# A graph layer on one core: additions behind chained operations, and two of ten step rows made by VectorE

## The reference

```python
q = (embeds[rows] @ qW).reshape(e, HEADS, dh)      # rows = src, cols = dst
k = (embeds[cols] @ kW).reshape(e, HEADS, dh)
v = (embeds[cols] @ vW).reshape(e, HEADS, dh)
scores = jnp.clip(jnp.einsum('ehd,ehd->eh', q, k), -10.0, 10.0)
exp_s = jnp.exp(scores)
norms = jax.ops.segment_sum(exp_s, rows, num_segments=nvar)[rows]
w = exp_s / (norms + 1e-08)
res = jax.ops.segment_sum(w[:, :, None] * v, rows, num_segments=nvar).reshape(nvar, d)
return embeds + res
# and outside: x = _layernorm(x + that, axis=-1)
```

## Time and profile before

| | |
|---|---|
| timed runs | 1259.94 us median of 3 (1259.18 to 1260.97) |
| profiled execution | span 1256.5 us; the page gives no other time for it |
| VectorE (DVE) busy | 1028.6 us, 82% |
| TensorE matmul (PE) busy | 976.0 us, 78% |
| GpSimd (POOL) busy | 866.1 us, 69% |
| ScalarE (ACT) busy | 656.4 us, 52% |
| gathers | 855, 986 ns mean |
| chain that ended last | DVE 25%, ACT 21%, POOL 20%, PE 17%, issue 13% |

### The profile page before, as it was taken

How to read it: one execution, slowest core, us unless ns; L and a number is a source line. 1 busy time by engine, 2 the same in 40 slices (tenths; PEclk the granted TensorE clock), 3 DMA queues, 4 the chain that set the end, 5 groups by cost and what they waited for, 6 DMA issues and landing times.

```text
span 1256.5 us, 23019 instructions
## 1 busy us (share of the span) xinstructions
PE 976.0 (78%) x6512; PEld 886.1 (71%) x6513; DVE 1028.6 (82%) x3053; ACT 656.4 (52%) x1469; POOL 866.1 (69%) x887
## 2 busy tenths in 40 slices
PE   8876788678776888776898777899777788888870
PEld 6765787568755788666888666788676777777760
DVE  8999998899898999889999789999668655555557
ACT  6852693249832499422899232799424322222225
POOL 1217776767777777777777777777777777777752
PEclk9996687659885599866799775799769755555555
DMA  6202222222222222222222222222622222222222
GB/s 174 88 10 76 77 80 69 74 64 75 78 73 70 70 75 79 76 74 68 77 77 80 78 75 70 79 77 78 151 79 80 77 78 78 79 78 77 77 61 77
DMA packets 67241, 98.34 MB, mean 78 GB/s; under 512 B 33127, under 2 KB 53204, under 8 KB 67134
## 3 DMA queue, kind: packets, MB, share of 16 engines
q0 software_dynamic: 41040, 84.10, 24.7%
q1 hardware_dynamic: 26094, 12.94, 3.9%
HBM read 89.77 MB, written 7.22 MB: 77 GB/s over the span
## 4 chain that ended last, share of the span: by engine, by line
DVE 25%; ACT 21%; POOL 20%; PE 17%; issue 13%; DVEq 2%; DMA 1%; SPq 0%; POOLq 0%; ACTq 0%
POOL kv L508 20%; ACT steps_m L719 14%; PE ps_r L662 5%; DVE acc L1127 4%; PE ps_q L648 4%; ACT oneh L773 3%; PE ps_a L631 3%; ACT onehT L767 2%; DVE steps_m L849 2%; DVE prod L1146 2%; DVE place_m L1013 2%; DVE place_m L1017 2%; DVEq L423 2%; PE ps_r L545 1%; DMA kv<-kv_table,dst_s 1%
## 5 line engine op out<-in xcount | busy, mean ns | idle before, releaser
L508 POOL DMA_INDIRECT kv<-kv_table,dst_s x855 | 843.4, 986 | 324.0 <-issue 315.8
L648 PE MATMUL ps_q<-qt,onehT 128*128 x1760 | 321.8, 348 | 108.6 <-ACT onehT L767 97.1
L648 PEld LDWEIGHTS ps_q<-qt,onehT 128*128 128x128 f32 x1760 | 291.3, 254 | 139.5 <-issue 139.0
L662 PE MATMUL ps_r<-wv,oneh 128*128 128x100 f32 x1752 | 322.5, 350 | 70.4 <-DVE wv L1156 69.9
L662 PEld LDWEIGHTS ps_r<-wv,oneh 128*128 128x128 f32 x1752 | 295.2, 258 | 87.0 <-DVE wv L1156 82.9
L719 ACT ACTIVATE steps_m<-iota_f,pos_t 125x254 f16<-125x254 f32 (+4 forms) x794 | 312.5, 502 | 16.4 <-PE ps_b L631 8.7
L1127 DVE TENSOR_TENSOR acc<-acc,ps_r 128x100 f32 x876 | 220.6, 252 | 62.9 <-issue 24.8
L767 ACT ACTIVATE onehT<-ps_t 128x640 f32<-128x640 bf16 x176 | 124.5, 707 | 183.2 <-PE ps_t L674 176.4
L760 ACT ACTIVATE wv<-clipped 128x20 f32<-128x20 f32 x176 | 39.4, 224 | 333.9 <-DVE clipped L1174 333.6
L631 PE MATMUL ps_a<-steps_m,place_m 125*128 125x254 f16 (+4 forms) x1504 | 183.9, 279 | 29.8 <-ACT steps_m L719 29.8
L1146 DVE TENSOR_TENSOR prod<-ps_q,kv 128x480 f32<-128x480 f32 x176 | 114.7, 652 | 107.3 <-DMA kv<-kv_table,dst_s 103.8
(11 more groups left out here) (208 smaller groups left out, 602.2 us busy)
## 6 DMA issues: line engine op xcount, KB each, us to landing
kv<-kv_table,dst_s POOLq DMA_INDIRECT x855
kv_table<-kv SPq DMA_DIRECT2D x7, 672.0 KB, 3.7
acc<-in_x_dram SPq DMA_DIRECT2D x6, 336.0 KB, 7.8
steps_m<-in_x_dram SPq DMA_DIRECT2D x6, 336.0 KB, 6.3
out_dram<-kv SPq DMA_DIRECT2D x6, 336.0 KB
dst_i<-in_dst_dram SPq DMA_DIRECT2D x1, 415.0 KB
src_i<-in_src_dram SPq DMA_DIRECT2D x1, 346.7 KB
acc<-in_x_dram SPq DMA_DIRECT2D x1, 288.0 KB, 4.6
```

Of the source, the lines that this page charges most:

```text
L508: nc.gpsimd.indirect_dma_start(kv[:, nm, u, :], None, kv_dram, bass.IndirectOffsetOnAxis(ap=dst_s[:, n * U + u:n * U + u + 1], axis=0)).th ...
L648: last = nc.tensor.matmul(ps_q[nm % 2][:, u * D:(u + 1) * D], onehT[:, nm % 2, u * P:(u + 1) * P], qt[:, bass.ds(blks[u], 1), :].rearrange ...
L662: last = nc.tensor.matmul(to, oneh[:, nm % 2, u, :], wv[:, nm % 2, u, :], start=True, stop=True)
```

## The change

In iterations with ranking pieces the pieces now run inside `tiles`: VectorE does product, weighing, reduction, one-hot and clip without any addition, then the pieces, and after each `link`'s instruction is issued, and before the wait for it, it issues one of the five additions (`add_one`); those left over come at the end. The register load of the block numbers moves ahead of the product in every iteration. `pair` and `select` wait only for what they read, over three buffers. `pay` moves into `count`, behind the counts' semaphore. The names of the pieces are spread over the iterations without `pay`. In iterations with a sort unit the third addition moves ahead of the clip, the fourth behind it, the fifth behind the one-hot. For groups 1 to 5 ScalarE makes eight Sign rows; VectorE makes the other two by a compare of 2 x (T + 1) elements (T is 204, 224, 243, 253, 253), payloads are doubled there too, and pos_h is made in each group.

```diff
+    KG = 2
@@ plan
-                    + ["pair0", "pair1", "pair2", "pay", "count", "base0", "base1", "bounds"]
+                    + ["pair0", "pair1", "pair2", "count", "base0", "base1", "bounds"]
...
             for k in range(ranked):
-                m = plan_iters(m, 1)
-                for name in names[at[k]:at[k + 1]]:
-                    PLAN.append(("piece", name, g))
+                m = plan_iters(m, 1, g, mid=names[at[k]:at[k + 1]])
@@ TensorE, unit
-                        steps = theta_d[:, vm, :, j] if g == 0 and j < KD else theta[:, vm, j, 0:w]
+                        steps = theta[:, vm, j, 0:w]
+                        if j < (KG if g else KD):
+                            steps = theta_g[:, vm, 0:w, j] if g else theta_d[:, vm, :, j]
@@ ScalarE
+            nc.scalar.activation(iota_g[:, :, :], iota_f[:, 0:TMAX + 1].unsqueeze(2).to_broadcast([P, TMAX + 1, KG]),
+                                 ACT.Copy)
...
-                for j in range(KD if g == 0 else 0, SU):
+                for j in range(KG if g else KD, SU):
@@ VectorE
-            def link(ins):
+            behind = [iter(())]
+
+            def step(ins):
 
                 own[0] += 1
                 ins.then_inc(s_own, 1)
+                return own[0]
+
+            def add_one():
+
+                for add_up, u in itertools.islice(behind[0], 1):
+                    add_up(u)
+
+            def link(ins):
+
+                step(ins)
+                add_one()
                 dve.wait_ge(s_own, own[0])
@@ pay
-                if g == 0:
-                    for part_of in (upper, lower):
-                        twice = part_of.rearrange("p (v c) -> p v c", c=SU)[:, :, 0:KD]
-                        link(nc.vector.tensor_scalar(twice, twice, 2.0, None, ALU.mult))
+                for part_of in (upper, lower):
+                    twice = part_of.rearrange("p (v c) -> p v c", c=SU)[:, :, 0:KG if g else KD]
+                    link(nc.vector.tensor_scalar(twice, twice, 2.0, None, ALU.mult))
@@ pair
+                a = 1 + 3 * i
                 if i == 0:
-                    link(nc.vector.tensor_scalar(rank_u[:, 0:K], bin_u[:, 0:K], 0.0, None, ALU.mult))
-                for d in range(1 + 3 * i, 4 + 3 * i):
...
+                    nc.vector.tensor_scalar(rank_u[:, 0:K], bin_u[:, 0:K], 0.0, None, ALU.mult)
+                known = compare(a)
+                add_one()
+                known_2 = compare(a + 1)
+                if i:
+                    dve.wait_ge(s_own, known)
+                    known = add(a)
+                add_one()
+                known_3 = compare(a + 2)
+                dve.wait_ge(s_own, max(known, known_2))
+                known = add(a + 1)
+                add_one()
+                dve.wait_ge(s_own, max(known, known_3))
+                known = add(a + 2)
+                add_one()
+                dve.wait_ge(s_own, known)
@@ count
                 nc.vector.tensor_copy(cnt[:, :], cnt_f[:, :]).then_inc(s_cnt, 1)
+                pay(g)
                 dve.wait_ge(s_pre, g + 1)
@@ base
+                if i:
+                    link(last)
+                else:
+                    add_one()
@@ select
+                def add(k):
+                    dve.wait_ge(s_own, max(chosen[0], chosen[k]))
+                    chosen[0] = step(nc.vector.tensor_tensor(rows(0), rows(0), rows(k), ALU.add))
+                    add_one()
+
+                chosen[i] = step(nc.vector.tensor_tensor(...))
+                add_one()
+                if i > 1:
+                    add(i - 1)
+                if i == 6:
+                    add(i)
+                    dve.wait_ge(s_own, chosen[0])
@@ own_position
-                if g == 0:
-                    link(nc.vector.tensor_scalar(pos_h[:, :], t, 0.5, None, ALU.add))
+                link(nc.vector.tensor_scalar(pos_h[:, 0:C], t, 0.5, None, ALU.add))
@@ unit
+                else:
+                    w = TS[g] + 1
+                    nc.vector.tensor_tensor(theta_g[:, vm, 0:w, :], iota_g[0:EP, 0:w, :],
+                                            pos_h[:, here].unsqueeze(1).to_broadcast([EP, w, SU])[:, :, 0:KG],
                                             ALU.is_le)
@@ tiles
+                if there(m - 2):
+                    blks = blocks_of(mybir.EngineType.DVE, m - 2)
                 multiply()
                 weigh()
                 if there(m - 2):
-                    blks = blocks_of(mybir.EngineType.DVE, m - 2)
                     dve.wait_ge(s_res, m - 2 + 1)
+                if mid:
+                    reduce()
+                    build()
+                    clip()
+                    behind[0] = iter([(add_up, u) for u in range(U)])
+                    for piece, g in mid:
+                        piece(g)
+                    for _, u in behind[0]:
+                        add_up(u)
+                    return
                 add_up(0)
                 reduce()
                 add_up(1)
                 build()
+                add_up(2)
                 clip()
-                add_up(2)
+                add_up(3)
                 if sorts:
-                    unit(*sorts[0], between=lambda i: add_up(3 + i))
+                    unit(*sorts[0], between=lambda i: None if i else add_up(4))
```

More of the change, by code:

```diff
@@ L3 @@
 from contextlib import ExitStack
+import itertools
 def gnn(nc, x, src, dst, qW, kW, vW, out):
@@ L85, in last_use, with plan_iters @@
         return MB + 2 * (k - MB) + 1 if k < MB + PAIRS // U else k + PAIRS // U
-    def plan_iters(m, count, units=()):
+    def plan_iters(m, count, g=0, units=(), mid=()):
         units = list(units) + [()] * (count - len(units))
-        PLAN.append(("iters", m, 0, units))
+        PLAN.append(("iters", m, g, units, mid))
         return m + count
@@ L131, in plan @@
             for k in range(ranked):
-                m = plan_iters(m, 1)
-                for name in names[at[k]:at[k + 1]]:
-                    PLAN.append(("piece", name, g))
+                m = plan_iters(m, 1, g, mid=names[at[k]:at[k + 1]])
             at = shares(units, count - ranked)
-            PLAN.append(("iters", m, g, [tuple(range(V0[g] + a, V0[g] + b)) for a, b in zip(at, at[1:])]))
+            m = plan_iters(m, count - ranked, g, [tuple(range(V0[g] + a, V0[g] + b)) for a, b in zip(at, at[1:])])
             PLAN.append(("piece", "lower", g))
-            m = plan_iters(m + count - ranked, 1)
+            m = plan_iters(m, 1)
             for name in ("differ", "turn", "choice"):
@@ L163, in gnn @@
         iota_s = sb("iota_s", [P, P, SU], f16)
-        pos_h = sb("pos_h", [EP, GC[0]], f16)
+        pos_h = sb("pos_h", [EP, CMAX], f16)
+        iota_g = sb("iota_g", [P, TMAX + 1, KG], f16)
+        theta_g = sb("theta_g", [EP, 2, TMAX + 1, KG], f16)
         iota_u = sb("iota_u", [P, NB], u16)
@@ L386, in follow @@
                 elif what[0] == "iters":
-                    _, m0, g, units = what
+                    _, m0, g, units, names = what
                     for k, vs in enumerate(units):
@@ L390, in follow @@
                         sorts = [(g, v - late, (v - late) % 2) for v in vs if V0[g] <= v - late < V0[g + 1]]
-                        tiles(m0 + k, (m0 + k) % R, sorts if unit else ())
+                        tiles(m0 + k, (m0 + k) % R, sorts if unit else (), [(pieces[p], g) for p in names if p in pieces])
                 elif what[2]:
@@ new lines, in add @@
+                def add(d):
+                    return step(nc.vector.tensor_tensor(rank_u[:, d * K:C], rank_u[:, d * K:C],
+                                                        same_u[:, d % 3, d * K:C], ALU.add))
+                a = 1 + 3 * i
+                if i == 0:
+                    nc.vector.tensor_scalar(rank_u[:, 0:K], bin_u[:, 0:K], 0.0, None, ALU.mult)
[5 more added lines that the diff above has]
+                    known = add(a)
@@ L1209, in tiles @@
                 else:
-                    add_up(3)
                     add_up(4)
-            follow(dve, tiles, unit, {"count": count, "table": table, "own": own_position, "pay": pay,
+            follow(dve, tiles, unit, {"count": count, "table": table, "own": own_position,
                                       "bounds": bounds, "choose": choose, "differ": differ, "pick": pick,
```

44 lines of the change are left out of this document (22 added, 22 removed).

## The result

The changed kernel takes 1249.83 us (median of 6, 1248.31 to 1251.50) against 1260.29 us for the kernel before in the same set (6 runs, 1256.80 to 1260.97): ratio 0.9924, 95% interval 0.9911 to 0.9936. Run again with the experiments it took 1251.98 us, ratio 0.9932 (0.9910 to 0.9954). The profiled execution took 1251.4 us with a span of 1249.6. Every execution whose span is listed took 1.8 us more than it, so the profiled one of the kernel before, with a span of 1256.5, took some 1258.3. The forecast was 1264.

What follows compares the result with a forecast made beforehand. Until 605 us VectorE's iteration time was taken to set the clock, afterwards GpSimd's gathers at 1.25 us each. Ranking -4.3, sort stages +5 and between stages +3 gave +4 on 1259.94: 1264 us, range 1249 to 1275.

Steps and rivals of the forecast that it cites:

- Ranking: VectorE's ranking iterations before 605 us: register load, additions and chains together save 4.3 us.
- (a): Ranking iterations before 605: the register load ahead of the product is no longer covered, net +16.5 us.
- (b): Ranking iterations before 605: additions placed in the waits of chained operations cost less, net -11.1 us.
- (c): Ranking chains before 605: removed waits, shorter pairs and moved payload, less new doublings and pos_h, net -9.7 us.
- Sort stages: Three sort stages before 605: VectorE's compare and closer additions, less waiting for ScalarE, add 5 us.
- slow step of four: First group's sort: strided matmuls 0.17 against 0.08 start to start; doubling would add 0.5 us per unit on TensorE, just hidden.
- Between the stages: After each sort: wait for cum_a stays, perhaps 0.3 shorter, and the register load costs more; three groups, +3 us.
- Rival 3: Sort stages and cum_a: ScalarE's relief reaches further, wait shrinks 1 to 2 us per group; -4, 1260 us; chance 0.20.
- what the change does to VectorE before 605 moves the end one for one: Before 605 us VectorE's time sets the clock, so its +4 us goes straight to the kernel's end.
- floor for stops: GpSimd's gaps above 0.30 us between gathers total 27 us at most, so no more can be won.
- a fixed 31 us: All 855 gathers: time taken beyond 0.95 us each, mean 986 against 0.95, 31 us in sum.
- the prediction's own key: If GpSimd's gaps above 0.30 vanish, the load or additions step failed; if they shrink with those right, sort stages were mis-sized.

Runs made afterwards that it cites:

- e3: Changed kernel with the register load back behind the weighing in iterations with ranking pieces: 1258.82 us (0.9983).
- e2: Kernel before with only the compare, its doubled payloads and pos_h; additions and register load as before: 1264.06 us (1.0024).
- e1: Changed kernel without the compare, ScalarE making all ten Sign rows; additions and register load stay changed: 1259.73 us (0.9987).
- e5: Changed kernel with the register load behind the weighing in ranking iterations and the selections chained again: 1242.12 us (0.9856).
- e10: Changed kernel, old sort-iteration addition order, weights copied to q's PSUM bank, TensorE waiting for the weighing, which still reads SBUF: 1277.29 us (1.0135).
- e14: Changed kernel, old sort-iteration addition order, weights copied to the transposes' PSUM bank, no new wait, weighing still reads SBUF: 1258.80 us (0.9982).
- e9: Changed kernel, old sort-iteration addition order, weighing reads weights copied to q's PSUM bank, TensorE waiting for the weighing: 1263.28 us (1.0024).
- e13: Changed kernel, old sort-iteration addition order, weighing reads weights copied to the transposes' PSUM bank, no new wait: 1239.80 us (0.9833).

## Why the prediction was wrong, step by step

**Up to iteration 71** VectorE was to lose 4 us; it won 9.7 (512.4 to 502.7 behind the first gather).

- Start: nothing forecast, -1.3 measured: the first product stands 8.8 us behind the first gather, not 10.1. What moved it is not settled.
- Ranking: -4.3 forecast, -5.4 measured. Its parts held nearly. The additions stand 0.40 apart. The load costs 1.33 or 1.34 us behind pieces that end in a chain (1.15 was taken), 1.07 behind serial additions (1.0), mostly nothing or 0.47 elsewhere. e3, which takes only the load back, has 12.9 us less in these iterations: so (a), forecast at +16.5, came to +12.9, and (b) and (c) together to -18.4 where -20.8 was forecast. Two errors cancelled in part. In the whole program the product's idle time has 46.5 us of issue in 49 places:

```profile
  DMA kv<-kv_table,dst_s: 91.2, 34
  issue: 46.5, 49
  PE ps_q L652: 14.2, 10
```

- Sort stages: +5 forecast, +4.1 measured. 5.8 per iteration of the fourth was forecast, 5.76 came, and the compare of 508 elements takes 0.42 us, as estimated. The strided matmuls cost nearly nothing: two of them start 0.24 us ahead of the plain ones (0.12 each), and the eight plain ones stand 0.11 apart (TensorE, fourth sort stage):

```profile
646.47 0.40 PE L635 MATMUL ps_a<-theta_g,place_m 125*128 125x254 f16 x2
646.71 1.04 PE L635 MATMUL ps_a<-steps_m,place_m 125*128 125x254 f16 x8
```

  The forecast had carried the slow step of four in the earlier trace rows over to a step of two, 0.5 us more on TensorE per unit; that was wrong, but hidden, and cost the sum nothing. The Trainium skill (Advanced Engine Details and Errata, SBUF Cachelines) asks for at least two hits on a 16-byte line. By that rule a step of two, with four hits, is free, and these rows agree; a step of four, with two, is not shown free by the earlier trace rows.

- **Between the stages: +3 forecast, -7.0 measured. This is the first step that failed.** It took the wait at cum_a for "the last unit on TensorE behind the last transposes". TensorE was itself waiting for ScalarE's last Sign row: in the changed kernel its last unit begins at 684.9, as ScalarE's last Sign row ends, and with two rows fewer per unit that is earlier. Behind the shorter wait the unit also kept the full granted clock, which no term and no rival had. Rival 3 had the first half of this mechanism, at -1 to -2 us per group; over the three groups it measured -9.5 alone (e2), and the +3 for the load and additions was right alone (e1: +3.7).

**From there to the end: "what the change does to VectorE before 605 moves the end one for one" is the second step that failed.** The floor for stops held (27 us at most, 20.6 won). But 15.2 of it came back as longer gathers, a term that stood in the sum as a fixed 31 us. With VectorE 9.7 us earlier at iteration 71 the last gather ended 5.5 earlier, both counted from the first gather. The two medians alone would have hidden this: they lie 10.5 apart, as if the end had followed one for one, and that is chance. The runs with one edit show the failure. In e1 and e2 VectorE is 8.0 and 7.6 us earlier than before, and the kernels are no faster. In e3 it is 23.5 earlier, the last gather 1.2 and the median 2.0 (1258.82 against 1260.84 beside it).

Had only the first step been right, the forecast would have been 1254, still 4 us above. The 10.5 us between the medians divide so: 5.5 from the first gather to the end of the last, 0.1 ahead of it, 1.2 behind it, and 3.6 because the profiled execution of the kernel before, at some 1258.3, is 2.0 below its median and that of the changed kernel 1.6 above. What makes one execution of a kernel longer than another no profile shows. A second profile of the changed kernel has excess 49.8 and stops 0.6, in sum 50.4 against 50.3.

**What was to show it:** Ahead of the product 1.1 us of idle time was expected, and none behind selections; it is 0 to 0.48 behind those of groups 2 and 3, but 1.06 or 1.07 behind all three of group 4, where left-over additions wait for one another last. The iteration with only tallies was to take 5 us and took 4.63. GpSimd's last stop was to be near 609, but ended at 561.52; its stops were to be above 25 us in sum, and are 2.3. By the prediction's own key vanished stops pointed at (a) or (b). Those two were nearly right: the key didn't allow for the 7 us won at cum_a.

## To carry to other kernels

Where GpSimd issues gathers at its own pace, their length is a term like any other: list those above the common length with what VectorE ran under them, and cost an edit by the VectorE operations with two SBUF inputs that it puts in a row or in step with them. Moving one small operand of such an operation to PSUM, in a bank that nobody must newly wait for, was worth 19 us here, about as much as all the rearranging up to e5 (18). And two edits with no gain each can have one together: test them apart and joined before dropping either.

## What the runs showed that was not expected

- A gather that starts under a VectorE operation with two SBUF inputs, 0.2 us or more ahead of its end, ends some 0.82 us behind that end (f32 weighing, bf16 one-hot, uint16 selection alike). Short gaps between such operations, filled with additions, don't let it in: up to 4.89 us in the changed kernel and 5.42 in e3.
- The group's marks, a compare of one uint16 input with a number, can hold a gather too, but mostly don't. Under the same 25 marks of the fifth group the kernel before has only gathers of 0.94 and 0.95 us, the changed one this. No run tells what decides it:

```profile
706.66 3.56 POOL L510 DMA_INDIRECT kv<-kv_table,dst_s  x1 [0.30 <-issue]
```
```profile
706.56 2.84 DVE L871 TENSOR_SCALAR steps_m<-bin_u 125x160 f16<-125x160 uint16 x25
```

- Two engines with their own periods can lock: 5.61 us of VectorE and four gathers with 0.61 of holding stayed in step for twelve of a sort stage's sixteen iterations, at 8 us for the stage (e2), and 0.15 us of idle time per iteration broke it.
- A wait of TensorE for an operation that it waits for anyway one step later cost 18 us (e10 against e14) and 23 (e9 against e13), since q then stood between the weighing and the sums that free GpSimd's buffers.
- Where TensorE waited 1.5 us instead of 3.1, it did the same twenty matmuls in 2.3 us instead of 4.0, at a granted clock of 1.00 instead of 0.57 (group 3's last unit).
